# A Perceiver block in two interleaved lanes: Pool waits, high parts first, halves, 1 MB tail loads, new merged orders

## The reference

```
x = x + xattn0(ln(x), ctx)      # 1 head, softmax over 257 context rows
x = x + attn0(ln(x))            # 16 heads of 16, causal
x = x + ffn0(ln(x))             # quantised gate/up/down, 256 -> 1024 -> 256
x = x + xattn1(ctx, ln(x))      # 16 heads, queries from x, keys and values from ctx
x = x + attn1(ln(x))            # 16 heads of 64
x = x + moe(ln(x))              # top 2 of 8 experts, and a shared expert (sw1, sw2, sw3)
```

## Time and profile before

| | |
|---|---|
| three runs, median | 2981.65 us (2981.3 to 2986.57) |
| profiled execution | 2995.97 us, span of its instructions 2993.7 us |
| PE, DVE, ACT, Pool busy | 80%, 61%, 40%, 16% of the span |
| mean granted TensorE clock | 0.942 of full speed |
| first stage, second stage, third stage, tail | about 63 to 1710, 1834 to 2640, 2640 to 2948, 2948 to 2994 us |

### The profile page before, as it was taken

One profiled execution on the slowest core, in us unless ns is written; L12 is line 12 of the kernel. 1 busy time (PEld: TensorE's weight loads), 2 busy tenths in 40 slices (PEclk: granted clock), 3 DMA queues, 4 the chain that ended last, 5 costly groups with the idle time before them and its releaser, 6 DMA issues.

```text
span 2993.7 us, 94094 instructions
## 1 busy us (share of the span) xinstructions
PE 2390.6 (80%) x35446; PEld 1819.3 (61%) x35479; DVE 1816.4 (61%) x4744; ACT 1208.3 (40%) x3016; POOL 493.8 (16%) x614
## 2 busy tenths in 40 slices
PE   2788888888888888888888867888888888758882
PEld 2565666666566666666666656666666666646661
DVE  4566666666666666666666664566555555545555
ACT  1445555555555555455554551222222222212220
POOL 2111111111111111111111111111111111112220
PEclk9899999999999999999999988999999999979996
DMA  5011111111111111111111122000000000112225
GB/s 195 28 42 56 42 56 34 49 49 42 56 42 56 34 50 49 42 56 42 56 33 42 57 93 87 14 16 14 14 16 16 16 16 16 66 50 67 67 67 193
DMA packets 86060, 152.29 MB, mean 51 GB/s; under 512 B 11224, under 2 KB 39904, under 8 KB 84576
## 3 DMA queue, kind: packets, MB, share of 16 engines
q1 hardware_dynamic: 73136, 117.81, 12.5%
q0 software_dynamic: 6528, 17.87, 1.6%
q10 hardware_dynamic: 6192, 13.38, 1.2%
HBM read 120.40 MB, written 28.62 MB: 50 GB/s over the span
## 4 chain that ended last, share of the span: by engine, by line
issue 50%; PE 24%; DVE 9%; POOL 7%; ACT 4%; DMA 3%; DVEq 2%; SPq 0%; POOLq 0%; ACTq 0%
PE ps L385 16%; POOL mem L469 3%; PE ps L1193 2%; PE ps L1508 2%; POOL x L1065 2%; POOL rstd L1059 1%; PE ps L1145 1%; DVEq L1486 1%; DVE mem L1377 1%; DVE mem L1556 1%; DMA y_tok<-mem 1%; DVE mem L1351 1%; DVE mem L1407 1%; DVE mem L1408 1%; DVE mem L1411 1%
## 5 line engine op out<-in xcount | busy, mean ns | idle before, releaser
L791 ACT ACTIVATE mem<-ps 128x512 f32<-128x512 f32 (+6 forms) x800 | 436.6, 559 | 543.5 <-PE ps L385 260.7
L385 PE MATMUL ps<-mem 128*128 128x256 f16 (+1 forms) x4224 | 557.4, 290 | 119.0 <-DVE mem L1377 79.6
L385 PEld LDWEIGHTS ps<-mem 128*128 128x128 f16 x4224 | 422.3, 103 | 221.8 <-DVE mem L1377 83.1
L385 PE MATMUL ps<-xt,mem 128*128 128x128 f16 x4608 | 281.4, 220 | 29.0 <-DVE xt L1332 29.0
L385 PEld LDWEIGHTS ps<-xt,mem 128*128 128x128 f16 x4608 | 262.3, 98 | 42.4 <-DVE xt L1332 38.9
L841 ACT ACTIVATE mem<-ps,neg_max 128x257 f32<-128x257 f32 x512 | 237.4, 476 | 71.4 <-DVE neg_max L1028 71.4
L1059 POOL TENSOR_TENSOR rstd<-var_eps,neg_half 128x1 f32<-128x1 f32 x128 | 70.1, 548 | 1002.4 <-DVE var_eps L895 1002.4
L469 POOL TENSOR_TENSOR mem<-mem 128x514 f16<-128x514 f32 x136 | 160.7, 1184 | 368.3 <-ACT mem L464 368.3
L1028 DVE TENSOR_REDUCE neg_max<-ps 128x2 f32<-128x514 f32 x256 | 173.5, 688 | 58.4 <-PE ps L686 54.5
L1508 PE MATMUL ps<-mem 128*128 x576 | 156.5, 395 | 35.2 <-ACT mem L1534 34.7
L699 PE MATMUL ps<-cst,mem 128*128 128x128 f32 x1024 | 159.4, 284 | 12.5 <-ACT mem L841 12.5
(11 more groups left out here) (252 smaller groups left out, 4252.1 us busy)
## 6 DMA issues: line engine op xcount, KB each, us to landing
mem<-in_ctx_t SPq DMA_DIRECT2D x136, 257.0 KB, 2.7
mem<-in_ctx_n SPq DMA_DIRECT2D x136, 256.0 KB, 3.3
mem<-x_sorted SPq DMA_DIRECT2D x74, 128.5 KB, 2.1
mem<-y_pairs SPq DMA_DIRECT2D x32, 256.0 KB, 3.9
mem<-in_experts ACTq DMA_DIRECT2D x7, 768.0 KB, 8.7
x<-in_x_tok SPq DMA_DIRECT2D x34, 128.0 KB, 2.9
x_mid<-x SPq DMA_DIRECT2D x32, 128.0 KB, 1.7
x<-x_mid SPq DMA_DIRECT2D x32, 128.0 KB, 2.0
```

The source lines that it names most:

```text
L385: last = pe.matmul(dst, a, b, start=i == 0 and j == 0, stop=i == n - 1 and j == 2)
L791: act.activation(dst, src, ACT.Copy).then_inc(*did(done))
```

## The change

1. **Pool waits.** After each `rstd` Pool also waits until DVE has written `xn`.
2. **High parts first.** xattn0's scores, attn1's query and key products and output product, and the shared expert's last product run all matmuls that need only high parts of the activations before those with low parts, and wait for the low parts in between.
3. **Halves in ffn0.** The quantised hidden row is made, transposed and copied in two halves of 512 columns.
4. **Tail.** The pair rows of a token lie so that 8 loads of 1 MB (runs of 8 KB) fetch them all; they are issued at once. DVE adds 1024 columns at a time, 8 stores of 512 KB follow. Before there were 32 loads of 256 KB (2 KB runs) in four slots and 32 stores of 128 KB.
5. **Orders.** All strings of the first stage, of the passage between the first two stages, and of the second stage but for ACT's and Pool's are new. The third stage's are as before. In xattn1 the last key's steps (`pl`, `last`, `rb`) move two value steps back.

```diff
-        tensor=("oooooyoyoyoyoooyooyoyoyooyoyyooyoooooyooyoooyoooooooooyoyyyoy"),
+        tensor=("oooooyoyoyyoyoyooyoyooyooyoyoyooyoyoyooooooooyooyyoooyyooooooo"),
...
+        def high_first(pe, groups, low_there):
+
+            for part in range(2):
+                if part == 1:
+                    low_there()
+                for n, (dst, terms) in enumerate(groups):
+                    for i, (stands, moves) in enumerate(terms):
+                        for a, b in ([(stands[0], moves[0]), (stands[1], moves[0])], [(stands[0], moves[1])])[part]:
+                            last = pe.matmul(dst, a, b, start=(part == 0 and n == 0 and i == 0 and a is stands[0]),
+                                             stop=(part == 1 and n == len(groups) - 1 and i == len(terms) - 1))
...
-                need("hq")
-                for k in range(8):
-                    last = pe.transpose(ps[:, 0, k * 64:(k + 1) * 64].bitcast(BF16), hq[:, k * P:(k + 1) * P], identb[:, :])
-                last.then_inc(*did("hq_ps"))
-                yield
+                for half in range(2):
+                    need("hq", half + 1)
+                    for k in range(4 * half, 4 * half + 4):
+                        last = pe.transpose(ps[:, half, (k % 4) * 64:(k % 4 + 1) * 64].bitcast(BF16), hq[:, k * P:(k + 1) * P], identb[:, :])
+                    last.then_inc(*did("hq_ps"))
+                    yield
...
-                yield from then(dve.tensor_scalar(rq3, r3, small[:, 15:16], ROUND, ALU.mult, ALU.add))
-                dve.tensor_scalar(hq, rq3, ROUND, 127.0, ALU.subtract, ALU.min).then_inc(*did("hq"))
-                yield
+                for i in range(2):
+                    cols = slice(512 * i, 512 * (i + 1))
+                    yield from then(dve.tensor_scalar(rq3[:, cols], r3[:, cols], small[:, 15:16], ROUND, ALU.mult, ALU.add))
+                    dve.tensor_scalar(hq[:, cols], rq3[:, cols], ROUND, 127.0, ALU.subtract, ALU.min).then_inc(*did("hq"))
+                    yield
...
                 pool.tensor_tensor(rstd[:, :], var_eps[:, :], neg_half[:, :], ALU.pow).then_inc(*did(f"ln_rstd{n}"))
+                pool.wait_ge(*at(t, f"xn{n}"))
                 yield
...
-                need("o5_lo", 2)
+                need("o5_lo", 1)
+                need("o5_hi", 2)
                 ao_hi, ao_lo = w2("ao", 8, D)
-                last = product(pe, ps[:, 0, 0:D], [((o5[:, 0, k], o5[:, 1, k]), (ao_hi[:, k], ao_lo[:, k])) for k in range(8)])
+                for part in range(2):
+                    if part == 1:
+                        need("o5_lo", 2)
+                    for k in range(8):
+                        for weight in (ao_hi, ao_lo)[0:2 - part]:
+                            last = pe.matmul(ps[:, 0, 0:D], o5[:, part, k], weight[:, k], start=(part == 0 and k == 0 and weight is ao_hi), stop=(part == 1 and k == 7))
...
+            by_token = pair_rows[0:PAIRS, :].rearrange("(p r) n -> p (r n)", p=P)
+            for g in range(OUT_GROUPS):
+                sp.dma_start(out_pair[g].rearrange("p s k n -> p (s k n)"), by_token[:, OUT_WORDS * g:OUT_WORDS * (g + 1)]).then_inc(s[f"pairs_in{g}"], 16)
+            sp.wait_ge(s["out_done"], 16 * OUT_GROUPS)
```

More of the change, by code:

```diff
@@ L85 @@
 PLAN_AT = W_COLS[1]
-OUT_SLOTS = 4
+OUT_GROUPS = 8
+OUT_TILES = TILES // OUT_GROUPS
+OUT_WORDS = OUT_TILES * 2 * D
+OUT_AT = [OUT_WORDS * g for g in range(W_COLS[1] // OUT_WORDS)]
+OUT_AT += [EXPERTS_AT + OUT_WORDS * g for g in range(OUT_GROUPS - len(OUT_AT))]
+assert OUT_AT[-1] + OUT_WORDS <= EXPERTS_AT + EXPERTS * E_WORDS
 MEM = ARENA_2[0] + LANE_2
@@ L550, in tensor1 @@
                 yield
-                need("q0_lo", 2)
+                need("q0_hi", 2)
                 need("tp_lo", NB)
-                for c in range(C):
-                    for a, r in ((0, 0), (0, 1), (1, 0)):
-                        for b in range(NB):
-                            last = pe.matmul(ps[SEQ * b:SEQ * (b + 1), 0, 0:KEYS], q0[:, a, c, SEQ * b:SEQ * (b + 1)], ctx_tp[:, r, c, b, :],
-                                             start=(c == 0 and a == 0 and r == 0), stop=(c == 1 and a == 1))
+                for a in range(2):
+                    if a == 1:
+                        need("q0_lo", 2)
+                    for c in range(C):
+                        for r in range(2 - a):
+                            for b in range(NB):
+                                last = pe.matmul(ps[SEQ * b:SEQ * (b + 1), 0, 0:KEYS], q0[:, a, c, SEQ * b:SEQ * (b + 1)], ctx_tp[:, r, c, b, :],
+                                                 start=(a == 0 and c == 0 and r == 0), stop=(a == 1 and c == 1))
                 last.then_inc(*did("s1_ps"))
                 yield
-                need("p1_last")
+                need("exps1")
                 for m in range(3):
+                    if m == 2:
+                        need("p1_last")
                     src = probs[:, m * P:(m + 1) * P] if m < 2 else last_cols[:, :]
@@ L851, in scalar2 @@
                 yield from v_out(1)
-                yield from act_copy(act, t, hqt.rearrange("p k n -> p (k n)"), ps[:, 0, :].bitcast(BF16), "hqt", "hq_ps")
+                for half in range(2):
+                    yield from act_copy(act, t, hqt[:, 4 * half:4 * half + 4].rearrange("p k n -> p (k n)"), ps[:, half, 0:D].bitcast(BF16), "hqt", "hq_ps", half + 1)
                 yield from v_out(2)
@@ L962, in vector1 @@
                 yield from then(dve.tensor_tensor(x[:, :], ps[:, 0, 0:D], x[:, :], ALU.add))
-                ins = yield from normalise(3, x[:, :])
-                yield from then(ins)
+                yield from normalised(3, x[:, :])
+                need("xn3")
                 yield from then(dve.tensor_reduce(small[:, 8:9], xn[:, :], X, ALU.max, apply_absolute_value=True))
@@ L999, in vector2 @@
                 need("ffn_y")
-                yield from then(dve.scalar_tensor_tensor(x[:, :], ps[:, 1, 0:D], small[:, 16:17], x[:, :], ALU.mult, ALU.add))
+                yield from then(dve.scalar_tensor_tensor(x[:, :], ps[:, 0, D:2 * D], small[:, 16:17], x[:, :], ALU.mult, ALU.add))
                 ins = yield from normalise(4, x[:, :])
@@ L1217, in tensor2 @@
                 yield
-                need("h_lo")
+                need("h_hi")
                 sw3_hi, sw3_lo = w2("sw3", 4, D)
-                last = product(pe, ps[:, 0, 0:D], [((h_p[:, 0, k * P:(k + 1) * P], h_p[:, 1, k * P:(k + 1) * P]), (sw3_hi[:, k], sw3_lo[:, k])) for k in range(4)])
+                for part in range(2):
+                    if part == 1:
+                        need("h_lo")
+                    for k in range(4):
+                        for weight in (sw3_hi, sw3_lo)[0:2 - part]:
+                            last = pe.matmul(ps[:, 0, 0:D], h_p[:, part, k * P:(k + 1) * P], weight[:, k], start=(part == 0 and k == 0 and weight is sw3_hi), stop=(part == 1 and k == 3))
                 last.then_inc(*did("z_ps"))
@@ L1637, in _ @@
                 sp.sem_inc(s[f"y_free{lane}"], 1)
-            for k in range(OUT_SLOTS):
-                sp.sem_inc(s[f"out_done{k}"], 1)
-            sp.sem_inc(s["out_pair"], OUT_SLOTS)
             sp.sem_inc(s["rows_given"], 1)
@@ L1755, in _ @@
             skewed("third", "scalar", act, third, E_TRIPS)
-            with act.Fori(0, TILES // OUT_SLOTS) as t:
-                for k in range(OUT_SLOTS):
-                    act.wait_ge(s["out_sum"], t * OUT_SLOTS + k + 1)
-                    act.dma_start(out[bass.ds(t * OUT_SLOTS + k, 1)].rearrange("t p d -> (t p) d"), out_sum[:, k]).then_inc(s[f"out_done{k}"], 16)
+            for g in range(OUT_GROUPS):
+                act.wait_ge(s["out_sum"], g + 1)
+                act.dma_start(out[:, OUT_TILES * D * g:OUT_TILES * D * (g + 1)], out_pair[g][:, :, 0, :]).then_inc(s["out_done"], 16)
         @block.tensor
```

96 lines of the change are left out of this document (48 added, 48 removed).

## The result

The changed kernel takes 3004.19 us, the median of eleven runs (2994.16 to 3012.72), against 2988.97 (2981.30 to 2995.19) for the kernel before in the same session: a ratio of 1.0049, 95% interval 1.0032 to 1.0066. It is slower, by 15 us where 45 were forecast.

A forecast was written before the change was run, and what follows sets the result against it. PE's work and waits were taken to bound the first two stages, DMA the tail. First stage +8 and +14, second +28, tail -5 sum to +45 on 2981.65: 3027 us, range 2955 to 3080.

The forecast's parts named there:

- What bounds the kernel: First two stages: PE's work plus the gaps in which it waits; tail: DMA, 45.8 us.
- Pool's wait: First stage: each `xn` that ran beside Pool's L469 comes 0.80 us earlier, which helps twice in a half.
- The new order, first stage: First stage: PE waits 8.65 us a half against 8.4, so the order gives back the edits' gain: +8 us.
- 1.45 in the cluster: First stage: PE's waits from the start of the softmax transposes to the end of DVE's L958, 1.45 us a half.
- The clock, first stage: First stage: loss at PE's lower clock rises from about 1.0 to 1.46 us a half: +14 us.
- Second stage: Second stage: PE's new waits of 4.95 us against 4.07 saved, +0.9 a half: +28 us, bounds +6 to +50.
- High parts first saves nothing more: Second stage: the product needs one low part and `xn` comes before both, so no further gain.
- Tail: Tail: faster pair-row loads -5.7, last group +1 to +2, four-slot turnarounds -1: -5 us, from 0 to -9.
- The wait behind the scores: Rival, first stage at L627: the wait put at 2.8 us is hidden; if nothing, 87 us less, 2940; chance 0.18.
- The clock does not get much worse in the first stage: Denies a rival: PE at 1.2 GHz through the whole wait cluster, loss up to 60 instead of 14, 3073; chance 0.13.
- stay up in the second: Rival, both stages: idle time is broken up and the lower clock is not granted, 2937; chance 0.08.
- Both signs: First stage: a PE wait at L627 under 1.5 us, or a mean clock above 0.98, would show the prediction wrong.

The follow-up runs named there:

- e11: e10 with 24 more idle products on PE in the first stage's wait behind the scores (L627): 2893.36 us, ratio 0.9671 to the kernel before.
- e12: e11 with 12 more idle products on PE in the first stage's wait at L809: 2839.41 us, ratio 0.9486 to the kernel before.
- e5: Changed kernel with the first stage's orders as before: 2995.84 us, ratio 1.0028 to the kernel before.
- e10: Changed kernel with old second-stage orders, landing awaited later and 14 idle products ahead of that stage's output product: 2868.11 us, ratio 0.9584 to before.
- e2: Changed kernel, but Pool waits for the scatter's landing only after the lane's next row statistic: 2916.48 us, ratio 0.9775 to the kernel before.
- e9: Kernel before, with 20 idle products on PE in the second stage's wait ahead of the output product: 2945.72 us, ratio 0.9845 to the kernel before.
- e8: Changed kernel with 24 idle products on PE ahead of the second stage's transposes of `xn`: 2946.84 us, ratio 0.9852 to the kernel before.
- e3: Kernel before with the new tail alone: 2978.51 us, ratio 0.9966 to the kernel before.

## Why the prediction was off

**What bounds the kernel.** Right: PE's work and its waits, stage by stage. The direction was right, and 3004 is within the range, but that is in part luck: both terms of the first stage had the wrong sign (+8 and +14 where -37 came of them together), the second stage's loss and the tail's gain were put too low, and these errors met with opposite signs. Of the 45 us forecast, 15 were measured.

**Pool's wait.** Right, and proved alone: 0.80 us an `xn` forecast, 0.77 and 0.51 found, 39 us over the stage in halves without a clock spell, 33 in the medians. I had given its gain away again in the next term.

**The new order, first stage: the step that failed.** "Sum after: 8.65 us against 8.4", "So the order gives back all that the edits win", +8 us. Step by step the walk was good: 2.8 and 1.8 forecast at the two new waits, 2.95 and 1.77 found, none at L765 and the first L390. But the many small ones were each put too high: 1.45 in the cluster became 0.81, 0.6 became 0.41, 0.8 became 0.52, 1.2 became about 0.8, so that the whole is 7.25 in place of 8.65, where before has 8.10 (and not the 8.4 that I had counted for it). Without clock spells a half takes 51.31 us before, and about 50.35 under the new order: 0.96 less, where I forecast 0.25 more. (The changed kernel has no half without a spell, so the 50.35 is that of e11 and e12, whose waits hold idle products; under the old order e5 has 50.33.) Times 31 this is -30 us in place of +8. The bound of 1 us to each side, -23 us at its lower end, did not reach that far: with some nine waits estimated one by one on the high side, the errors add up. The premise was wrong as well: as far as e5 shows, the edits other than Pool's win nothing, and the order gives nothing back.

**The clock, first stage.** "+14 us": wrong in sign. A half loses 52.60 - 51.31 = 1.29 us to it before, where I had 1.0, and 51.36 - 50.35 = 1.01 after, where I had 1.46. And yet the clock fell, from 0.97 to 0.95. 30 of the 31 spells now begin at L627, right behind the wait of 2.95 us, and lie over small steps and the wait of 0.81 us: L636 takes 1.09 us in place of 0.84, and only the longer spells reach L422 (2.08 us in place of 1.03). Before, most lay over L392, full of work. I had carried the loss behind a wait from the second stage over to a place where something else stands behind the wait. e11 measures it directly: 24 products in that wait lift the clock to 0.98 and win 0.25 us a half; with e12's 12 more at L809 it is 0.99, and 0.80 us are won (51.41 in e10, 50.61 in e12).

**Second stage.** "+28 us", from waits alone: 4.95 forecast against 4.07. Measured are 4.96 against 4.38, +17 us. The chain cast, scatter, landing, `rstd`, `xn`, transposes is as forecast (PE's wait 4.1 forecast, 4.07 found; e2 proves the landing). Two things were left out. The clock loss behind that wait rises from 1.50 (e9) to 2.08 us (e8), another 17 us (0.26 us a half are in neither), which stood in my bound and not in my sum, though I had used the very row for the first stage. And "High parts first saves nothing more" holds only as the order stands: it wins 1.32 us a half once PE does not wait for `xn` first. The stage and its end came out at +41.2 and +7.7; the first is inside the bound of +6 to +50, the second was not forecast (some 5 us of it are the border's, see the result).

**Tail.** -5 forecast, -10.2 found (e3: -10.8 of time). The loads' rate was right (24.7 and 25.2 KB/us): over the whole tail they took 58.3% of 45.9 us before and 59.3% of 35.7 after, 5.6 us less, where -5.7 was forecast. The stores took 26.3% and 33.2%, 0.2 us less. The rest is time in which the engines moved nothing, 15.4% of 45.9 us and 7.5% of 35.7: 4.4 us less. There I had put -1 us for the four slots and +1 to +2 for the last group.

**Rivals.** The wait behind the scores is not hidden (2.96 us). The clock does not get much worse in the first stage, nor stay up in the second. Both signs that I had named as proof against me (L627 under 1.5 us, a clock above 0.98) stayed away, and the first-stage terms were still wrong by 60 us: they tested the two large waits, not the sum.

**The sum.** In the traces: -37.2 - 3.0 + 41.2 + 7.7 - 10.2, with +0.1 ahead of the first stage, is -1.4 us. The medians say +15. What differs between executions was not pursued; in which stretch the others lose their 17 us stays open.

## What to carry to other kernels

Look at what is behind a wait, not only at how long it is: the same two or three microseconds cost their own length, plus the clock for the work that follows. In the first stage a spell of the shorter kind cost 1.4 to 1.7 us over the dense product L392 and 0.5 to 0.8 over small steps and a wait. A mean granted clock ranks two kernels only if it falls over the same work. In an order written out by hand, ask of each step that is moved to the front what the engine that feeds it has ahead of it: here Pool held a wait for a DMA that nobody needed for another half, and the new order made PE wait for it; to move that wait won 2.5 us in each half. And where a wait can't be removed, idle products in it can pay: 57, 48 and 46 us here in e8, e9 and e10.

## What the hardware showed beside that

**A standstill that comes and goes with code elsewhere.** 24 added matmuls in the first stage made PE stand still for 2.15 us in every second half of the second stage, and in just that stretch the queue for instructions moved 109 packets (1.79 MB), none in e10 and e12, whose second-stage code is the same. The nearest reading is that the code of PE's loop was fetched anew in e11 and not in the others; where the code lay was not measured. A fetch by itself is not enough: in the first stage all kernels have some 165 such packets and hardly a standstill of this kind. The Trainium skill (Runtime: NRT & Kernel Launch, Instruction fetch mechanics) says that a taken branch whose target is not at hand forces a fetch ahead of execution; the rows agree, in that each standstill stands behind the loop's branch with such a packet beside it, and the price was 33 us. So a change of a few instructions moved the time by 1% with no wait of its own.

**Clock and time are not in step.** Among the halves of the changed kernel's first stage, those with one spell of the shorter kind take 50.9 to 51.2 us and those with one of twice its length 51.5 to 51.8, against 50.35 without. Before, one of the shorter kind made 52.7 to 53.0 of 51.31.
